# A graph network of a GRU layer and three GIN layers on one core: semaphore increments by pairs of cells, by units and by blocks of nine row tiles

## The reference

```python
def _layernorm(x, axis=-1, eps=1e-05): ...                 # (x - mean) / sqrt(var + eps)
# first layer
src_h = h[src] @ W_msg.T + b_msg
msg = src_h + edge_embed[edge_type]
messages = segment_sum(msg, dst)
h_new = _gru_cell(messages, h, W_ih, W_hh, b_ih, b_hh)     # two sigmoid gates and a tanh
x = _layernorm(x + h_new)
# GIN layers, three times (the first adds ee, the others put it beside the source row)
ee = edge_attr @ enc_w + enc_b
agg = segment_sum(concat(h[src], ee) or h[src] + ee, dst)  # with self loops
h = relu(_bn_eval(agg @ w1 + b1)) @ w2 + b2
# at the end
x = _layernorm(x + h)
```

## Time and profile before

| | |
|---|---|
| median of 3 runs (lowest to highest) | 9094.97 us (9082.56 to 9097.97) |
| the profiled execution | 9098.04 us, of which the span is 9096.2 us |
| mean granted clock of TensorE | 0.824 of full speed |
| busy: PE, DVE, ACT, POOL | 67%, 38%, 16%, 52% of the span |
| stages | 3513, 1514, 1342 and 2704 us |

### The profile page before, as it was taken

One profiled execution on the slowest core, in us unless ns is written; L12 is line 12 of the kernel. 1 busy time (PEld: TensorE's weight loads), 2 busy tenths in 40 slices (PEclk: granted clock), 3 DMA queues, 4 the chain that ended last, 5 costly groups with the idle time before them and its releaser, 6 DMA issues. The chain is left out here.

```text
span 9096.2 us, 88724 instructions
## 1 busy us (share of the span) xinstructions
PE 6077.8 (67%) x28807; PEld 2856.9 (31%) x28807; DVE 3476.6 (38%) x14291; ACT 1489.0 (16%) x2862; POOL 4775.4 (52%) x4959
## 2 busy tenths in 40 slices
PE   3354546454554533555555799899898988888888
PEld 1122212121221211232223344444344444344343
DVE  7354535354453533344434444444221212222222
ACT  1122212132222311111112222222000000000000
POOL 5543343434434354544453566666666666666664
PEclk9876767676776766766667899999999999999999
DMA  6265646475665654322222677777776777776775
GB/s 205 57 146 123 155 110 164 111 175 125 161 143 137 157 129 101 83 73 76 77 80 67 199 230 216 220 229 228 222 215 200 223 213 212 233 207 204 208 212 177
DMA packets 1390704, 1478.16 MB, mean 163 GB/s; under 512 B 818695, under 2 KB 1131926, under 8 KB 1390246
## 3 DMA queue, kind: packets, MB, share of 16 engines
q1 hardware_dynamic: 1177750, 1123.36, 43.7%
q0 software_dynamic: 212496, 349.08, 15.2%
HBM read 1024.47 MB, written 280.48 MB: 143 GB/s over the span
## 5 line engine op out<-in xcount | busy, mean ns | idle before, releaser
L2768 POOL DMA_INDIRECT GL<-h_gathered,IDXA x2646 | 2562.0, 968 | 1529.4 <-issue 703.5
L2690 PE MATMUL ps<-MS,HP 128*128 128x512 bf16 (+1 forms) x11700 | 2829.4, 385 | 84.1 <-issue 58.3
L2735 POOL DMA_INDIRECT rec_q<-BIG x1563 | 1503.6, 962 | 1999.6 <-DVE BIG L1821 1505.5
L2475 PE MATMUL ps<-MT,XPS 128*128 128x512 bf16 x3822 | 1173.3, 421 | 1307.4 <-issue 931.6
L2690 PEld LDWEIGHTS ps<-MS,HP 128*128 128x128 bf16 x11700 | 1160.8, 101 | 1397.1 <-issue 323.8
L2253 ACT CAST MT<-ps 128x512 bf16<-128x512 f32 x1274 | 736.4, 586 | 2466.3 <-remote 1320.1
L2750 POOL DMA_INDIRECT BIG<-x_parts,SRCq x739 | 704.8, 954 | 740.7 <-PE ps L2572 452.3
L2475 PEld LDWEIGHTS ps<-MT,XPS 128*128 128x128 bf16 x3822 | 381.6, 104 | 1886.7 <-issue 1121.6
L2081 DVE TENSOR_REDUCE ROW<-ps 128x128 f32<-128x384 f32 x294 | 163.0, 554 | 1740.0 <-remote 858.6
L1871 DVE CAST CAR<-ps 128x98 f16<-128x98 f32 x429 | 109.2, 255 | 1722.5 <-remote 1343.7
L2660 PE MATMUL ps<-GL,SL 128*128 128x384 bf16 (+1 forms) x2646 | 613.5, 341 | 37.5 <-issue 37.0
(11 more groups left out here) (225 smaller groups left out, 4959.3 us busy)
## 6 DMA issues: line engine op xcount, KB each, us to landing
MS<-counts SPq DMA_DIRECT2D x936, 512.0 KB
counts<-BIG SPq DMA_DIRECT2D x312, 512.0 KB
XPS<-x_parts SPq DMA_DIRECT2D x168, 384.0 KB
GL<-h_gathered,IDXA POOLq DMA_INDIRECT x2646
rec_q<-BIG POOLq DMA_INDIRECT x1563
rec_q<-BIG SPq DMA_DIRECT2D x44, 490.0 KB, 10.9
HTI<-h_cols SPq DMA_DIRECT2D x72, 256.0 KB
RECL<-rec_q SPq DMA_DIRECT2D x24, 520.0 KB
```

The costliest lines, as they stand in the source:

```text
L2475: got = t.matmul(PS[6 + x.j % 2][:, :], XPS[:, x.load % 3, i, part, :], MT[:, m % 3, 512 * i:512 * (i + 1)], start=4 * x.u + i + part == 0 ...
L2690: got = t.matmul(bank[:, 0:w].rearrange("p (b c) -> p b c", c=P), HP[:, d, part, :], MS[:, i % MR, 0:x.nb, d % MB, :], start=d + part == 0 ...
L2735: g.indirect_dma_start(out=RAd, out_offset=bass.IndirectOffsetOnAxis(ap=POSI[:, c:c + 1], axis=0), in_=RECA[q % 3][:, c - a, :], in_offset ...
L2768: g.indirect_dma_start(out=GL[:, r % LR, i, 0:3 * P], out_offset=None, in_=HGd[lay], in_offset=bass.IndirectOffsetOnAxis(ap=IDXA[:, a + i: ...
```

## The change

Increments become fewer, and each wait is moved to the next increment that is left.

- Cells go in pairs: PE does two cells, then the sums of the pair before. `mt` and `mt_out` come once a pair, `xd` once a unit. DVE's increments for the one-hots of a unit (one for all `OHS`, one for each `OHD`) become one, `made`.
- Rank groups: the ring `OH` has four places and DVE makes one-hots three groups ahead; `hot` is counted for the first three groups alone. `car` is gone; the `SELH` matmul waits for the product, which DVE does behind the carry's copy. The increments of some DVE operations on the window's places are gone.
- First layer: one `q0_hot` a slot, and `q0_sum` only at odd `q`. A wait for an even one waits for the next slot that signals (`summed`).
- Layers: `row_hot`, `row_attr` and `row_sum` come once a block of nine row tiles, the ring has 12 row groups, and POOL waits once a block for the block four back. ACT's attribute copies go by blocks (98 of 128x9x51 in place of 294 of 128x3x51). `ER` is gone and `RECL` is overwritten in its place.

```diff
-LR = 10
+LR = 12
...
+LB = LR // KQ
...
+def signals(q):
+    return q % 2 == 1 or q == NQ0 - 1
+def summed(k):
+    return sum(signals(s[0]) for s in SLOTS[:k + 1] if s[0] is not None) + (not signals(SLOTS[k][0]))
...
         def rank_onehot(v, w, i):
             g = w.g0 + i
-            if g >= 3:
-                v.wait_ge(rank.sem, g - 2)
+            if g >= 4:
+                v.wait_ge(rank.sem, g - 3)
...
-            got.then_inc(*hot.inc())
+            if g < 3:
+                got.then_inc(*hot.inc())
...
             if m >= 3:
-                v.wait_ge(mt.sem, cells_to(m - 3))
+                v.wait_ge(mt.sem, cells_to(m - 3) // 2)
             for i in range(x.n):
-                got = v.tensor_scalar(OHS[m % 3][:, i, :], I132[:, :, 0:44], RECS[k % 2][:, par, x.at + i, 1:2], None, ALU.is_equal)
-            got.then_inc(*ohs.inc())
+                v.tensor_scalar(OHS[m % 3][:, i, :], I132[:, :, 0:44], RECS[k % 2][:, par, x.at + i, 1:2], None, ALU.is_equal)
...
+            got.then_inc(*made.inc())
...
-                        v.tensor_copy(CAR[:, g % 2, :], PS[g % 2][:, (GT - 1) * NB:GT * NB]).then_inc(*car.inc())
+                        v.tensor_copy(CAR[:, g % 2, :], PS[g % 2][:, (GT - 1) * NB:GT * NB])
...
             elif dense is not None:
                 r = q - QS0
                 if r >= QR:
-                    v.wait_ge(q0_sum.sem, GATHERED[q - QR] + 1)
+                    v.wait_ge(q0_sum.sem, summed(GATHERED[q - QR]))
...
             for i in range(x.n):
                 c = x.c0 + i
-                s.wait_ge(mt.sem, c + 1)
-                s.copy(MT[:, m % 3, 512 * i:512 * (i + 1)], PS[2 + c % 4][:, :]).then_inc(*mt_out.inc())
+                if c % 2 == 0:
+                    s.wait_ge(mt.sem, c // 2 + 1)
+                got = s.copy(MT[:, m % 3, 512 * i:512 * (i + 1)], PS[2 + c % 4][:, :])
+                if c % 2 == 1:
+                    got.then_inc(*mt_out.inc())
...
             if not fresh:
-                t.wait_ge(car.sem, CARRY[g - 1][1])
+                t.wait_ge(prod.sem, g)
...
-                t.wait_ge(ohd.sem, c + 1)
                 if c >= 4:
-                    t.wait_ge(mt_out.sem, c - 3)
-                t.matmul(PS[2 + c % 4][:, :], OHS[m % 3][:, i, 0:P], OHD[c % 8][:, 0:512], start=True, stop=True).then_inc(*mt.inc())
+                    t.wait_ge(mt_out.sem, c // 2 - 1)
+                t.matmul(PS[2 + c % 4][:, :], OHS[m % 3][:, i, 0:P], OHD[c % 8][:, 0:512], start=True, stop=True)
+                t.matmul(PS[3 + c % 4][:, :], OHS[m % 3][:, i + 1, 0:P], OHD[(c + 1) % 8][:, 0:512], start=True, stop=True).then_inc(*mt.inc())
                 if c >= 2:
                     sums_tensor(t, c - 2)
+                    sums_tensor(t, c - 1)
...
-            got.then_inc(*xd.inc())
+            if i == x.n - 1:
+                got.then_inc(*xd.inc())
...
             for i in range(LT):
                 got = t.matmul(bank[:, 0:w], SL[:, r % LR, i, :], GL[:, r % LR, i, 0:w], start=at + i == 0,
                                stop=at == KQ - 1 and i == LT - 1, skip_group_check=True)
-            got.then_inc(*row_sum.inc())
+            if at == KQ - 1:
+                got.then_inc(*row_sum.inc())
...
-                        if r >= LR:
-                            g.wait_ge(row_sum.sem, r - LR + 1)
+                        if r >= LR and r % KQ == 0:
+                            g.wait_ge(row_sum.sem, r // KQ - LB + 1)
```

More of the change, by code:

```diff
@@ L148, in carries @@
 def carries():
-    on, n = [], 0
+    on = []
     for w in WIN:
         for i in range(w.groups):
-            last = i == w.groups - 1 and (w.q + 1 >= 25 or WIN[w.q + 1].fresh)
-            n += 0 if last else 1
-            on.append((not last, n))
+            on.append(not (i == w.groups - 1 and (w.q + 1 >= 25 or WIN[w.q + 1].fresh)))
     return on
@@ L1837, in cells_vector @@
                 if k >= 2:
-                    v.wait_ge(ohd.sem, cells_to(last_unit(lambda y: y.half == k - 2)))
+                    v.wait_ge(made.sem, last_unit(lambda y: y.half == k - 2) + 1)
                 w = 4 * HU if k % 2 == 0 else NB - 4 * HU
@@ L2353, in row_attrs_scalar @@
         def row_attrs_scalar(s, upto):
-            while attrs_so_far[0] < min(upto, QL):
-                r = attrs_so_far[0]
-                x = group_of(r)
-                at = BD + LT * (r - x.group0)
+            while attrs_so_far[0] < min(upto, NB):
+                n = attrs_so_far[0]
+                x = group_of(KQ * n)
+                at, slot = BD + K * (n - x.block0), KQ * (n % LB)
                 s.wait_ge(ea3.sem, x.k + 1)
-                if r >= LR:
-                    s.wait_ge(row_sum.sem, r - LR + 1)
-                s.copy(GL[:, r % LR, :, 3 * P:XC], EAP[:, x.k % 2, at:at + LT, :, :].rearrange("p c r k -> p c (r k)")).then_inc(*row_attr.inc())
+                if n >= LB:
+                    s.wait_ge(row_sum.sem, n - LB + 1)
+                s.copy(GL[:, slot:slot + KQ, :, :].rearrange("p q i w -> p (q i) w")[:, :, 3 * P:XC],
+                       EAP[:, x.k % 2, at:at + K, :, :].rearrange("p c r k -> p c (r k)")).then_inc(*row_attr.inc())
                 attrs_so_far[0] += 1
@@ L2369, in layer_scalar @@
             if k and before < SG:
-                s.wait_ge(attr_all.sem, GRP[before].block0 + GRP[before].nb)
+                s.wait_ge(attr_all.sem, k)
                 if before >= 2:
@@ L2548, in first_counted @@
             n, r, k, at = tiles_of(q, C), q % DR, (q + 2) // 4, (q + 2) % 4
-            t.wait_ge(q0_hot.sem, 2 * (COUNTED[q] + 1))
+            t.wait_ge(q0_hot.sem, COUNTED[q] + 1)
             if q == 0:
@@ L2788, in cell_records_sync @@
             if k >= 2:
-                y.wait_ge(ohs.sem, last_unit(lambda z: z.half == k - 2) + 1)
+                y.wait_ge(made.sem, last_unit(lambda z: z.half == k - 2) + 1)
             at, w = (0, 4 * HU) if k % 2 == 0 else (4 * HU, NB - 4 * HU)
```

120 lines of the change are left out of this document (60 added, 60 removed).

## The result

The changed kernel takes 9397.8 us (median of 4 runs, 9377.6 to 9413.6), the kernel before 9088.8 us beside it: a ratio of 1.034, 95% interval 1.032 to 1.036. The forecast was 9055 us, within 8830 to 9190. The profiled execution has a span of 9375.8 us. Of all the executions behind this text one, of the kernel before, fell into a slower state (10,647 us, granted clock 0.77) and is left out.

The account below looks back on a forecast made before the run. Took late-seen PE increments during POOL's DMA bursts as the kernel's one large store of time. Sum: 9098 + 5 (sort) + 28 (first layer) − 70 (layers 1, 2) + 0 = 9061, less 3, rounded to 9055 us; range 8830 to 9190.

Parts of the forecast that it names:

- What bounds the kernel: Sort stage: PE's increments reach other engines late while POOL issues DMAs; 21 bursts of some 80 us, 1700 us in all.
- Increments or matmuls: Sort-stage bursts: delay counted by matmul (2.7, 3.2, 2.7 us), not by increment, so fewer increments gain 0 in a burst.
- Rival B: Sort-stage bursts: delay counted by increments, so fewer of them gain 217 us, 8838 us in all; chance 0.15.
- Sort stage: Whole stage: 0 in bursts and +5 us for the rest, bounds 0 to 20; stage ends at 3513 within 20 us.
- The terms for `SELH` and `made`: Sort stage: `SELH` about 0.5 us later per rank group, `made` some 1.6 us later; nothing in bursts, mostly covered elsewhere.
- First layer: DVE's one-hots wait longer, so `sum` comes 1.07 us later at 25 idle places: +28 us, bounds 0 and twice that.
- GIN layers 1 and 2: Step falls from 54.1 to 52.7 us, the mean of 50.5 and 54.85: −70 us, bounds −180 and +40.
- floor: GIN layers 1 and 2: a step without turn stalls or half-clock loss takes 54.1 − 5.3 − 3.2 = 45.6 us.
- the clock term: GIN layers 1 and 2: half-clock loss falls from 3.2 us a step to about 1.7, one stretch at half clock.
- Runs of 18 in half of the steps: GIN layers 1 and 2: POOL runs nine DMAs into the next nine without a pause in about half the steps; 54.85 us each.
- Rival C: GIN layers 1 and 2: POOL never pauses at c2's end, every step 54.85 us, +40; 9168 us in all; chance 0.22.
- GIN layer 0: Same cycle as layers 1 and 2 with less clock lost; 0 us, from −35 to +35.

## Why the prediction was wrong

- **What bounds the kernel: right in kind.** I put the store at 1700 us of the sort stage. Breaking the runs gave back 848 us there and 322 in the first layer. The chip without the delay takes 1385 us less for the sort stage (with the memsets in it), so 1700 was too high; in all it takes 2500 us less, so much of the store lay in the other stages, for which I had no figure. That the whole difference between the chips is this delay is argued, not shown.
- **Increments or matmuls: right.** Pairs came 19.9 us apart where I had said 21 to 22, rank groups 14.0. Rival B (8838 us) is out.
- **Sort stage, +5 forecast, +39 measured.** The terms for `SELH` and `made` took the bursts as neutral and the rest as covered; with the bursts broken the part costs nothing that can be told, so the 39 us are in the bursts. A mis-sized term, over its upper bound of 20.
- **First layer, +28 forecast, +30 measured** (33 to 39 between other pairs of traces that differ in it). The step was 25 idle places of `sum` times a slot's one-hots of 1.07 us. The trace agrees in kind: DVE's idle time for PE has moved from `sum` (now 20.3 us, 12 times, where the earlier trace rows has 57.4 and 25) to the one-hots ahead, for which the kernel before has no such row:

```profile
DVE BIG L2013 <- PE ps L2570: 105.0, 38, 7.1
```

  These are 38 places where I had counted 25, and no run has this part alone, so the price of a place isn't shown; that the number fits so well may be luck.
- **GIN layers 1 and 2, −70 forecast, +170 measured: the step that failed.** My sum for a step was a floor of 45.6 us, 5.4 for stalls ahead of the turn (the mean of 3.2 and 7.55) and 1.7 for the clock. The stalls came better than that: 2.9 us a step, from 5.3. What failed is the floor, with the clock term on it. The floor let PE run free between turns at any age of POOL's run; but in runs of 18 DMAs, and in pairs of nine with 1.4 us between, PE's own matmuls come at about a third of their pace behind an age of 15 us or more. That is 3.9 us a step of idle time where the kernel before has 0.3 (the row above, of which I took no note): +3.5. And the clock loss, which I let fall from 3.2 to 1.7 us a step, rose: PE's busy time grew by 1.8 us a step where I had booked −1.5, and the half clock stands right behind these stalls. Against the forecast step of 52.7 us these are −2.5, +3.5 and +3.3, some 4.3 of the 4.9 us that are missing.
- **Runs of 18 in half of the steps:** 20 in 50 steps. Rival C (9168 us) had the right place and sign, longer runs of POOL, but +73 us where +309 were measured, by the same omission; and it put its cost on the turn, where the changed kernel gained.
- **GIN layer 0, 0 forecast, +41 measured,** just over the bound of 35. The ring of 12 and the attributes by blocks, with POOL's fine wait, stand at 21 us below the kernel before; POOL's coarse wait takes 45 to 62.
- The range failed with this: its upper end was built from rival C's price.

Open: why the delay exists on some chips and not on another; what makes POOL's run hold PE at all; which coarse wait of the sort stage costs the 39 us; whether a pause has to be long or has to see the landing; and whether ring and pauses together beat the pauses alone (7921 us), since that kernel has a time only where nothing is late.

## What to carry to other kernels

On some chips long runs of indirect DMAs on GpSimd can hold back what TensorE has finished, and in still longer runs its own issue. Look for "remote" waits whose work was long done, and lay them beside the age of POOL's run. The remedy that worked is a wait for a landing after six to eight DMAs where POOL has time to spare (−13% here with six, in two stages), not fewer increments; a coarser wait ahead of the DMAs makes it worse, since it joins runs. When you judge a run, look at the pause ahead of it too: a short one does not start the count again. And measure on more than one chip: where nothing is late, the same pauses cost 12%.

## What the runs showed of the hardware

- Everywhere but on one chip the kernel before took about 9090 us, on that chip 6575 us, with the same program and operations of the same length. I had not expected a chip to differ by 28%.
- While POOL issued indirect DMAs 1.26 us apart, ACT saw cells of four matmuls 10.84 us apart, pairs of eight 19.92, and DVE saw rank groups of five 13.30 to 14.00: 2.5 to 2.8 us a matmul, whatever the number of increments.
- In layers 1 and 2, behind an age of 15 us or more of a run of 18 DMAs, or of two of nine with 1.4 us between, dense 128x512 matmuls with nothing to wait for started about 0.7 us apart rather than 0.22. Of runs of nine behind a longer pause, 2 of 118 stalled PE by more than 0.8 us.
- A gap of 0.4 us behind every six DMAs freed nothing. A pause of 1.4 us was enough behind six DMAs (one late release behind 68 of them), and not behind eight (40 behind 57) or twelve (53 behind 85). Runs of six and eight scatters gave a sort stage of 2663 and 2715 us, of twelve 3271, of 64 3511.
